# Key-mask tests split between products and maxima, and two stretches of a two-layer attention and expert kernel put in another order

## The chip, the cores and the metric

The kernel runs on one core of a Trainium2 chip. The metric is the device time of one execution in microseconds (us); lower is better. Shown are the median of three runs and one profiled execution.

## The reference

The input x holds 2 batches of 512 rows of 256 numbers, the context 2 batches of 1024 rows. Four steps follow each other, each added to x:

```python
x = x + attention0(layernorm(x), ctx, ctx, mask0, ...)   # 16 heads of 16, scores masked with -inf, softmax
x = x + experts0(layernorm(x), ...)                      # the best of 8 experts (256 -> 512 -> 256, GELU)
x = x + attention1(layernorm(x), ctx, ctx, mask1, ...)   # queries, keys, values normalised; bias -1e9 if masked
x = x + experts1(layernorm(x), ...)                      # shared expert (704 wide, SiLU) + the best 2 of 7
```

mask0 is 512 x 1024 int32, the same for both batches. mask1 is 2 x 512 x 1024, one byte each. In the inputs at hand both are nonzero for keys at the end of the context alone, the same for all 512 queries: keys 0 to 767 are masked away for every query (their entries are zero), and of the last 256 some are kept.

## The kernel before

All five engines run one program written out by hand: semaphores alone order them, and each engine and each DMA queue (SP's and ACT's) goes through its own list in order.

**Fast path and proof.** The kernel starts on the assumption that only the last FK = 256 keys of each batch count. While it computes, it proves this from the masks: `onesb` (all ones) times the mask rows on TensorE gives, for each key, how many of the 512 queries see it. The counts of keys 0 to 767 must be zero, those of the last 256 either 0 or 512 (`u = (512 - c) * c` must be zero), and some key must be left. The result is the flag on which all engines branch after step 3 of layer 0 (`branch`); in these inputs the fast path goes on.

**Start** (`sp_start`, `act_start`, `pe_start`, `dve_start`). SP's and ACT's queues issue the loads: halves of the keys `CTf` (ct_0, ct_1, 256 KB each), x tiles 0 to 3 (x0) and 4 to 7 (x1), weights `WP` (Wk, Wv, Wq), `cols` (14 KB), mask0 in two halves (m0_0, m0_1, 1 MB each), mask1 (1 MB). TensorE projects keys, turns the normalised x, projects queries and values, and counts mask0 in four plus four products of 512 columns (L524). VectorE does the statistics of x0, normalises two tiles, makes six small constants, casts both halves of mask0 to ones (L818), copies a turned half (L798) between the two, then does the statistics of x1, the values, and the row of mask values (`mval0`, L809) that SP spreads into `KT` (L589). `pe_first` begins with the scores (L890); it waits for `kt`, that row (`masked`) and `compact(1, 1)`.

**Attention** runs in 8 steps a layer, of 8 heads-by-batches each (`pe_step`, `dve_step`, `act_step`), every step in four gaps. In each step TensorE makes scores for the next step's maxima (L890), scores turned the other way for the exponentials (L900) and outputs (L921); VectorE takes 8 maxima (L1093), adds one turned maximum (L1099) and divides (L1107); ACT takes exponentials (L1260). The maxima go through a ring of three PSUM banks (`m_claim`: TensorE may write one when VectorE has freed the one three uses before). Other work is put beside: in layer 0 the counts of mask1, two products of 4 x 512 columns in each of steps 1 and 2 (`count0_0` to `count1_1`, L524), read by `dve_counts`; ACT's casts of mask1 (L704); and small VectorE work in pieces after each maximum (`late`): `key_counts_rest` for mask0 in step 1, for mask1 in steps 2 and 3.

**Shared expert of layer 1** (`shared_pe`, `shared_act`, `shared_dve`). It runs in CHUNKS = 12 chunks n, six to a batch: `shared_up(n)` (L1916), SiLU on ACT (L1946), the product on VectorE (`mul`, L1961), `shared_down(n - 1)` (L1927). The routing of the 7 experts is put beside the chunks (`beside1(n)` of the three engines): the last output of attention, statistics, turned rows, logits (L1579), `choose_experts`, ranks, `gates1`, `places1`, `tables1`. After the places POOL scatters the rows (16 indirect DMAs, L1747). Then come 19 tiles of routed experts (`tiles1`: up L2007, down L2022), whose up-weights SP loads (`load_up`, 1.4 MB each, three buffers) before it loads the scattered rows (`load_x`, L2797).

Of the kernel before, what the change touches and what calls it, by code (L numbers as in the profile page):

```python
# [5 lines left out]
F32 = mybir.dt.float32  # L6
# [11 lines left out]
NB = 2  # L18
# [40 lines left out]
def build(nc, A, out):  # L59
# [80 lines left out]
    fsum = sb("fsum", [128, 12], F32)  # L140
    junk = sb("junk", [128, 1], F32)
# [98 lines left out]
    def bank_uses():  # L240
        six, seven = [], []
        after = (["close1", "project1", "rows0_1", "x1_0", "q1_0"], ["rows1_1"])
        for l in range(NB):
# [12 lines left out]
            if l == 0:  # L256
# [13 lines left out]
    BESIDE_M = {(0, 0, 1): ["wg"], (0, 1, 1): ["count0_0"], (0, 1, 3): ["count0_1"], (0, 2, 1): ["count1_0"],  # L270
                (0, 2, 3): ["count1_1"], (0, 5, 1): ["close0_1"], (0, 5, 3): ["project0_0", "project0_1"],
# [249 lines left out]
    def key_counts_half(bank, b, mu, hf):  # L521

        for q in range(4):
            m = pe.matmul(PS[:, bank, :], onesb[:, :], mu[:, b * 4 + q, hf * 512:(hf + 1) * 512],  # L524
                          start=(q == 0), stop=(q == 3))
        return m

    def key_counts_pe(b, mu):

        key_counts_half(6, b, mu, 0)  # L530
        return key_counts_half(7, b, mu, 1)

    def key_counts_dve(n, c):

        flat = PS[:, 6:8, :].rearrange("p a n -> p (a n)")
        dve.tensor_reduce(fsum[:, n:n + 1], flat[:, 0:3 * FK], AX, ALU.add).then_inc(sem("counted"), 1)
        dve.tensor_copy(c, flat[:, 3 * FK:SK]).then_inc(sem("counted"), 1)

    def key_counts_rest(v, n, c, u):

        some, left, both = fsum[:, n:n + 1], fsum[:, 4 + n:5 + n], fsum[:, 7:8]
# [4 lines left out]
        settle(v, dve.tensor_reduce(fsum[:, 3:4], u, AX, ALU.add))  # L546
        yield
        settle(v, dve.tensor_tensor(some, some, fsum[:, 3:4], ALU.add))
        settle(v, dve.tensor_scalar(some, some, 0.0, None, ALU.is_equal))
        yield  # L550
        settle(v, dve.tensor_scalar(left, left, 0.0, None, ALU.is_gt))
        settle(v, dve.tensor_tensor(some, some, left, ALU.mult))
        if n:
            settle(v, dve.tensor_tensor(both, both, some, ALU.mult))
        else:
            settle(v, dve.tensor_copy(both, some))
        if n == 2:
            dve.tensor_copy(flags[:, 0:1], both).then_inc(sem("flag"), 1)
# [18 lines left out]
    def sp_start():  # L577
        load_keys0(sp, 0)
        sp.dma_start(X[:, 0:2, :], x_v[:, 0:2, :]).then_inc(sem("x0"), 16)
        sp.dma_start(WP[:, 1, :, :], A["L0_xattn_WvT"].rearrange("(k p) n -> p k n", p=128)).then_inc(sem("wp_1"), 16)  # L580
        load_mask0(sp, 0)
        sp.dma_start(X[:, 4:8, :], x_v[:, 4:8, :]).then_inc(sem("x1"), 16)
# [64 lines left out]
    def act_start():  # L647
        act.dma_start(WP[:, 0, :, :], A["L0_xattn_WkT"].rearrange("(k p) n -> p k n", p=128)).then_inc(sem("wp_0"), 16)
        act.dma_start(X[:, 2:4, :], x_v[:, 2:4, :]).then_inc(sem("x0"), 16)
        act.dma_start(cols[:, :, :], A["cols"]).then_inc(sem("col"), 16)  # L650
        load_keys0(act, 1)
        load_mask0(act, 1)
        act.dma_start(WP[:, 2, :, :], A["L0_xattn_WqT"].rearrange("(k p) n -> p k n", p=128)).then_inc(sem("wp_2"), 16)
# [4 lines left out]
        keys_compact(0)  # L658
# [3 lines left out]
        keys_compact(1)  # L662
# [18 lines left out]
        for f in range(2):  # L681
            queries_compact(2 + f, 3 + f)
            mask_cast(2 * f, 2 * f + 2)
# [18 lines left out]
    def mask_cast(q0, q1):  # L702
        for q in range(q0, q1):
            act.activation(mu1[:, q, :], m1i[:, q, :], ACT.Copy).then_inc(sem("mu1"), 1)  # L704
# [23 lines left out]
    def pe_start():  # L728
# [6 lines left out]
        def values_pair(j0):  # L735
            for j in (j0, j0 + 1):
                m = projected(4 + j // 2, j, 1, CTf, KCOLS[j])
            m.then_inc(sem("vals_ps"), 1)
# [5 lines left out]
        for b in range(NB):  # L744
            pe.wait_ge(sem(f"ct_{b}"), 16)
            for f in range(2):
                m = keys_half(f, b)
                if b:
                    m.then_inc(sem("k_ps"), 1)
        pe.wait_ge(sem("consts"), CONSTS)  # L750
# [3 lines left out]
        pe.wait_ge(*at(0, "wp_1", 16))  # L754
        values_pair(0)
# [3 lines left out]
        projected_T(0, 2, 0, XT[:, :, 0:512]).then_inc(sem("q_ps"), 1)  # L759
        pe.wait_ge(sem("mu0"), 2)  # L760
        key_counts_pe(0, mu0).then_inc(sem("count"), 1)
        projected_T(1, 2, 1, XT[:, :, 0:512]).then_inc(sem("q_ps"), 1)
        values_pair(2)

    def turn_second():

        pe.wait_ge(*at(0, "xn", 8))
        pe.wait_ge(sem("counted"), 3)
# [12 lines left out]
    def dve_start():  # L781
# [5 lines left out]
        for i in (0, 1):  # L787
            normal_dve("x0_0", i, XN[:, i, :], X[:, i, :]).then_inc(sem("xn"), 1)
        dve.wait_ge(sem("col"), 16)
# [2107 lines left out]
```

## Time and profile before

| | us |
|---|---|
| median of 3 runs | 516.57 (514.02 to 517.53) |
| the profiled execution | 517.48 |
| its span, first to last instruction | 516.2 |
| TensorE busy | 491.3 (95%) |
| VectorE busy | 258.8 (50%) |
| ACT busy | 201.4 (39%) |

Busy shares are means over stages with different limits. "idle before <-X" says how long the engine stood still before an instruction and whose end released it. Windows are in us from the start of the span. A matmul on float32 stands as two entries, so x8 are four matmuls.

### The profile page before, as it was taken

What the parts mean: (1) busy time and instruction counts of PE and PEld (TensorE: products, weight loads), DVE (VectorE), ACT (ScalarE), POOL (GpSimd) and SP (SyncE); (2) the same over time, 40 slices, a digit from 0 to 9 for tenths busy, and PEclk for the clock granted to TensorE, in tenths of its full rate; (3) what the DMA queues carried; (4) which work ended last, traced back from release to release, by engine and by line L of the source; (5) the groups of instructions that cost most, each with busy time, mean ns of one, the idle gap of its engine ahead of it and who ended that gap; (6) DMA issues with size and microseconds to landing.
All of it is one profiled execution on the core that took longest, in us unless ns stands there. A gap on an engine that the chain in (4) does not pass through costs nothing.

```text
span 516.2 us, 8825 instructions
## 1 busy us (share of the span) xinstructions
PE 491.3 (95%) x3290; PEld 368.5 (71%) x3293; DVE 258.8 (50%) x776; ACT 201.4 (39%) x416; POOL 85.2 (17%) x124
## 2 busy tenths in 40 slices
PE   6999999999999999999999899998999999999994
PEld 4555545648999887654654366565989999999993
DVE  4678897764474753876679352711313223223220
ACT  3747546452646445446465522301222222222221
POOL 2246000004020200200000000272021221221122
PEclk9999999999999999999999999998999999999999
DMA  8820009995132310480000300097676676676612
GB/s 297 237 66 2 2 13 341 367 356 180 42 102 64 102 32 22 125 283 2 1 0 2 117 6 1 21 360 247 223 260 184 228 254 190 220 257 191 218 21 27
DMA packets 43383, 73.13 MB, mean 142 GB/s; under 512 B 3553, under 2 KB 33729, under 8 KB 43332
## 3 DMA queue, kind: packets, MB, share of 16 engines
q1 hardware_dynamic: 34580, 60.47, 34.8%
q0 software_dynamic: 4336, 6.75, 5.9%
q10 hardware_dynamic: 4416, 5.26, 3.2%
q8 instruction: 29, 0.48, 0.4%
q14 instruction: 22, 0.18, 0.1%
HBM read 56.35 MB, written 14.51 MB: 137 GB/s over the span
## 4 chain that ended last, share of the span: by engine, by line
PE 78%; DVE 11%; DMA 5%; issue 2%; ACT 2%; POOL 1%; ACTq 0%; POOLq 0%; DVEq 0%
PE PS L2007 17%; PE PS L2022 9%; PE PS L890 9%; PE PS L1916 6%; PE PS L900 6%; PE PS L1789 5%; PE PS L1802 5%; PE PS L1927 4%; PE PS L921 3%; PE PS L402 3%; DVE W L1093 3%; PE PS L376 2%; DMA CT<-in_ctxT 2%; PE PS L909 2%; PE PS L381 1%
## 5 line engine op out<-in xcount | busy, mean ns | idle before, releaser
L1093 DVE TENSOR_REDUCE W<-PS 128x2 f32<-128x512 f32 x128 | 83.7, 686 | 34.8 <-PE PS L890 34.0
L2007 PE MATMUL PS<-PR,W 128*128 128x128 f32 x836 | 96.5, 275 | 0.0
L2007 PEld LDWEIGHTS PS<-PR,W 128*128 128x128 f32 x836 | 94.9, 192 | 0.1
L890 PE MATMUL PS<-W 32*128 32x256 f32 x512 | 83.1, 399 | 2.2 <-DVE W L1093 1.9
L900 PE MATMUL PS<-W 32*128 32x512 f32 x256 | 78.7, 638 | 0.2
L890 PEld LDWEIGHTS PS<-W 32*128 32x128 f32 x512 | 55.1, 184 | 24.8 <-issue 11.2
L2022 PE MATMUL PS<-W,PR 128*128 x228 | 52.5, 380 | 0.8 <-ACT PR L2739 0.8
L2790 POOL DMA_INDIRECT out<-PR,slots x19 | 29.7, 1563 | 131.9 <-ACT PR L2739 128.8
L1260 ACT ACTIVATE PR<-PS 128x512 f32<-128x512 f32 x64 | 35.2, 596 | 32.5 <-PE PS L900 32.4
L2022 PEld LDWEIGHTS PS<-W,PR 128*128 128x128 f32 x228 | 41.9, 190 | 6.1 <-issue 1.2
L1260 ACT ACTIVATE W<-PS 128x512 f32<-128x512 f32 x64 | 34.5, 598 | 22.0 <-PE PS L900 21.8
L2043 DVE TENSOR_TENSOR PR<-PR,PS 128x512 f32<-128x512 f32 x19 | 13.1, 688 | 58.8 <-PE PS L2007 58.8
L1916 PE MATMUL PS<-XT,W 128*128 128x512 f32 x88 | 40.1, 596 | 0.0
L900 PEld LDWEIGHTS PS<-W 32*128 32x128 f32 x256 | 24.1, 183 | 13.3 <-issue 6.6
L1789 PE MATMUL PS<-PR,W 128*128 128x128 f32 x256 | 31.6, 275 | 0.0
L1802 PE MATMUL PS<-W,PR 128*128 128x256 f32 x128 | 31.0, 382 | 0.0
L1789 PEld LDWEIGHTS PS<-PR,W 128*128 128x128 f32 x256 | 30.0, 192 | 0.3 <-issue 0.3
L1916 PEld LDWEIGHTS PS<-XT,W 128*128 128x128 f32 x88 | 16.2, 190 | 16.5 <-issue 16.1
L1927 PE MATMUL PS<-W,PR 128*128 128x256 f32 x96 | 24.4, 399 | 2.9 <-DVE PR L1961 1.9
L1927 PEld LDWEIGHTS PS<-W,PR 128*128 128x128 f32 x96 | 19.0, 200 | 11.0 <-issue 5.8
L1833 ACT ACTIVATE PR<-PS,b1c 128x128 f32<-128x128 f32 x64 | 18.3, 368 | 19.9 <-PE PS L1789 14.8
L1802 PEld LDWEIGHTS PS<-W,PR 128*128 128x128 f32 x128 | 23.0, 190 | 3.4 <-issue 1.0
(274 smaller groups left out, 591.0 us busy)
## 6 DMA issues: line engine op xcount, KB each, us to landing
W<-in_rguT SPq DMA_DIRECT2D x19, 1408.0 KB
W<-in_L_ffn_W SPq DMA_DIRECT2D x16, 512.0 KB, 9.6
W<-in_rdT SPq DMA_DIRECT2D x5, 768.0 KB, 11.2
scratch_rows<-W SPq DMA_DIRECT2D x1, 2860.0 KB
VR<-scratch_rows SPq DMA_DIRECT2D x19, 130.0 KB, 5.4
W<-in_mask SPq DMA_DIRECT2D x2, 1024.0 KB, 12.4
scratch_x<-W SPq DMA_DIRECT2D x1, 2048.0 KB, 14.2
PR<-scratch_x SPq DMA_DIRECT2D x16, 128.0 KB, 2.2
```

What stands on the lines that cost most here:

```text
L890: m = pe.matmul(PS[:, bank, q * FK:(q + 1) * FK], QT[r:r + 32, g, c:c + 128], KT[r:r + 32, g, b * FK:(b + 1) * FK], start=True, stop=True)
L900: pe.matmul(PS[:, bank, :], KT[r:r + 32, g, b * FK + kb * 128:b * FK + (kb + 1) * 128], QT[r:r + 32, g, 512 * b:512 * (b + 1)], start=True ...
L1093: dve.tensor_reduce(NM[:, s % 2, q:q + 2, c], PS[:, m_bank(use), :].rearrange("p (q n) -> p q n", q=2), AX, ALU.max).then_inc(sem("m_free" ...
L1260: act.activation(PX[s % 2][:, HEADS_W[k], :], PS[:, e_bank(use), :], ACT.Exp).then_inc(sem("e_free"), 1)
L1789: m = pe.matmul(PS[:, up_bank(i), j * 128:(j + 1) * 128], W[:, o:o + 128], XS0[:, i % 2, k, :], start=(k == 0), stop=(k == 1))
L1802: pe.matmul(PS[:, bk, 0:D], HT0[:, i % 2, j, :], W[:, o:o + D], start=(j == 0), stop=False)
L1833: act.activation(HT0[:, i % 2, j, :], PS[:, up_bank(i), j * 128:(j + 1) * 128], ACT.Gelu, bias=b1c[:, c:c + 1]).then_inc(sem("gelu"), 1)
L1916: m = pe.matmul(PS[:, 2 * (n % 2) + w, :], W[:, k * 2 * F1 + o:k * 2 * F1 + o + 128], XT[:, k, 512 * b:512 * b + 512], start=(k == 0), sto ...
L1927: m = pe.matmul(half(4 + t // 2, t), HS[:, n % 2, t * 128:(t + 1) * 128], W[:, o:o + D], start=(j == 0 and t % 2 == 0), stop=(j == NJ1 - 1 ...
L2007: m = pe.matmul(PS[:, bank, j * 128:(j + 1) * 128], W[:, o:o + 128], XS[:, r % 2, k, :], start=(k == 0), stop=(k == 1))
L2022: m = pe.matmul(PS[:, 6, 0:D], HT[:, r % 2, j, :], W[:, bass.ds(slot * SLOT + o, D)], start=(j == 0), stop=(j == NJ1 - 1))
L2790: ins = pool.indirect_dma_start(out, off, YO[:, r % 2, :], None, compute_op=ALU.add)
```

## The change

Three parts.

1. **Masks.** The products count the last 256 keys alone: mask0 in 4 products of 256 columns instead of 8 of 512, mask1 in 8 products of 256 columns in one place, step 2 gap 1 (`counts`), instead of 16 of 512 in four places. Keys 0 to 767 are tested on VectorE by maxima over the raw masks read as 32-bit words: 768 words of each of mask0's four row groups (two in the start, two in step 1), and 4 x 192 words for each batch of mask1 (step 1). 12 maxima a partition are made 0 or 1024 and join the counts by one more product, which adds to all counts and so breaks the test if any is nonzero. The casts shrink with the products: VectorE's to 2 x 256 numbers each, ACT's from eight of 1024 bytes to two of 4 x 256, both in the start. The small work on mask1 runs once, on 2 x 256 numbers, in step 3.
2. **Start.** SP's queue: ct_0, x tiles 0 and 1, ct_1, x1, m0_0. ACT's: Wk, cols, x tiles 2 and 3, Wv, Wq, m0_1. ACT normalises before it copies the projected keys. VectorE takes the statistics of x1 and copies the turned half before it casts masks. The values are projected one by one between other work. `turn_second` no longer waits for the counts to be read; `pe_first` does, later.
3. **Shared expert of layer 1.** The division of step 6 comes before chunk 0's product; the turned rows, logits and ranks of batch 1 move up by one chunk, `tables1` stays at chunk 5, after the places at 4. SP's second `load_up` waits for product 8, the third comes after the scattered rows' first two loads.

```diff
-    BESIDE_M = {(0, 0, 1): ["wg"], (0, 1, 1): ["count0_0"], (0, 1, 3): ["count0_1"], (0, 2, 1): ["count1_0"],
-                (0, 2, 3): ["count1_1"], (0, 5, 1): ["close0_1"], ...
+    BESIDE_M = {(0, 0, 1): ["wg"], (0, 2, 1): ["counts"], (0, 5, 1): ["close0_1"], ...
...
+    def key_counts(bank, c, mu, q0):
         for q in range(4):
+            m = pe.matmul(PS[:, bank, c:c + FK], onesb[:, :], mu[:, q0 + q, :], start=(q == 0), stop=(q == 3))
...
+    def first_keys0(v, q):
+        dve.tensor_reduce(first[:, q:q + 1], m0w[:, q, 0:SK - FK], AX, ALU.max).then_inc(*v.up())
+    def first_keys1(v, b):
+        dve.tensor_reduce(first[:, 4 + 4 * b:8 + 4 * b], m1w[:, 4 * b:4 * b + 4, 0:(SK - FK) // 4], AX, ALU.max).then_inc(*v.up())
+    def first_keys_late(v):
+        for q in (2, 3):
+            first_keys0(v, q)
+            yield
+        dve.wait_ge(sem("m1"), 16)
+        for b in range(NB):
+            first_keys1(v, b)
+            yield
+        dve.wait_ge(*v.now())
+        dve.tensor_scalar(firstb[:, :], first[:, :], 0.0, 1024.0, ALU.not_equal, ALU.mult).then_inc(sem("first_keys"), 1)
+        yield
+        yield from keys_alike(v, mc[0], mt[0], 0)
+    def keys_known(v):
+        dve.wait_ge(*m_freed("counts"))
+        yield from keys_alike(v, mc[1], mt[1], 1)
...
     def sp_start():
         load_keys0(sp, 0)
         sp.dma_start(X[:, 0:2, :], ...)
-        sp.dma_start(WP[:, 1, :, :], A["L0_xattn_WvT"]...)
+        load_keys0(sp, 1)
+        sp.dma_start(X[:, 4:8, :], x_v[:, 4:8, :]).then_inc(sem("x1"), 16)
         load_mask0(sp, 0)
-        sp.dma_start(X[:, 4:8, :], x_v[:, 4:8, :]).then_inc(sem("x1"), 16)
...
     def act_start():
...
-        keys_compact(0)
         act.wait_ge(sem("stats"), NORMS[True]["x0_0"])
         for i in (2, 3):
             normal_act("x0_0", i, XN[:, i, :], X[:, i, :]).then_inc(sem("xn"), 1)
-        keys_compact(1)
+        for f in range(2):
+            keys_compact(f)
...
+            elif (n, gap) == (2, 1):
+                pe.wait_ge(sem("mu1"), NB)
+                pe.wait_ge(sem("first_keys"), 1)
+                bank = m_claim("counts")
+                for b in range(NB):
+                    key_counts(bank, b * FK, mu1, 4 * b)
+                pe.matmul(PS[:, bank, 0:12], onesb[:, :], firstb[:, :], start=False, stop=True, ...
...
-            late = counts_rest(v, s - 2) if s > 1 else key_counts_rest(v, 0, mc[0][:, 0, :], mt[0]) if s else iter(())
+            late = first_keys_late(v) if s == 1 else keys_known(v) if s == 3 else iter(())
...
         def beside1(n):          # VectorE; TensorE and ACT move with it
             if n == 0:
-                dve_divide(1, 6, v)
                 dve_divide(1, 7, v)
...
-            elif n == 3:
+            elif n == 2:
                 dve_xt("rows1_1", 1)
-            elif n == 4:
+            elif n == 3:
                 ... logits1_1, choose_experts(v, 2)
-            elif n == 5:
+            elif n == 4:
                 gates1(v)
                 ... places1(v, ...)
+            elif n == 5:
                 whole(tables1(v))
+        dve_divide(1, 6, v)
         shared_dve(beside1)
...
-            for r in range(UPS):
-                load_up(r)
+            load_up(0)
+            sp.wait_ge(sem("mul"), CHUNKS - 4)
+            load_up(1)
             sp.wait_ge(sem("scattered"), SCATTERED[2])
             load_x(0)
             load_x(1)
+            load_up(2)
```

## Rows read from the trace of the kernel before

**Rows 1.** The page's chain that ended last, share of the span by engine.
```profile
PE 78%; DVE 11%; DMA 5%; issue 2%; ACT 2%; POOL 1%; ACTq 0%; POOLq 0%; DVEq 0%
```

**Rows 2.** Windows of all engines: busy us (x instructions), PEclk, DMA share, GB/s.
```profile
48.18:54.25 6.07, 5.82 (x44) 3.25 (x48) 5.83 (x15) 4.09 (x8) 4.72 (x7) 1.00 0.00 0
54.25:59.18 4.93, 4.93 (x45) 2.58 (x48) 3.80 (x10) 2.10 (x5) 0.00 (x0) 1.00 0.01 2
79.24:83.20 3.96, 3.96 (x40) 2.21 (x44) 3.75 (x7) 2.88 (x6) 0.00 (x0) 1.00 0.96 301
```

**Rows 3.** Windows of VectorE alone, from a step's first maximum to the next step's.
```profile
46.30:57.10 10.80, 9.63 (x21) 1.00 0.00 1
57.10:68.10 11.00, 9.82 (x24) 1.00 0.01 1
68.10:77.29 9.19, 8.53 (x22) 1.00 0.05 13
```

**Rows 4.** DMA issues of the start: KB each, us from issue to landing.
```profile
X<-in_x SPq DMA_DIRECT2D x1, 512.0 KB, 13.4
WP<-in_L_xattn_WvT SPq DMA_DIRECT2D x1, 256.0 KB, 6.2
CT<-in_ctxT ACTq DMA_DIRECT2D x1, 256.0 KB, 8.8
```

**Rows 5.** Timeline of the start: start us, us, instruction, idle before.
```profile
5.64 3.78 PE L731 MATMUL PS<-CT,WP 128*128 128x256 f32 x8 [1.68 <-DMA WP<-in_L_xattn_WkT]
...
11.20 1.99 PE L731 MATMUL PS<-CT,WP 128*128 128x256 f32 x8 [1.78 <-DMA CT<-in_ctxT]
...
12.95 1.08 ACT L473 ACTIVATE PR<-X,NW 128x256 f32<-128x256 f32 x2
...
16.81 1.88 PE L381 MATMUL PS<-XT,WP 128*128 128x512 f32 x4
...
20.91 0.72 SPq L589 DMA_DIRECT2D W<-W  x1
...
23.99 1.14 PE L890 MATMUL PS<-W 32*128 32x256 f32 x8
```

**Rows 6.** VectorE up to 80 us by line and form: count, busy us, mean ns.
```profile
L818 DVE TENSOR_SCALAR W<-W 128x2048 bf16<-128x2048 int32 x2 | 2.4, 1219 | 0.0
L546 DVE TENSOR_REDUCE fsum<-W 128x1 f32<-128x256 f32 x3 | 1.3, 420 | 0.1
L536 DVE TENSOR_REDUCE fsum<-PS 128x1 f32<-128x768 f32 x1 | 0.9, 947 | 0.0
```

**Rows 7.** Timeline of the shared expert of layer 1.
```profile
296.07 0.63 PE L934 MATMUL PS<-ident,W 128*128 128x128 f32 x4 [1.57 <-DVE W L1107]
...
334.94 2.93 SPq L515 DMA_DIRECT2D W<-in_rguT  x3
...
335.38 1.97 PE L1927 MATMUL PS<-W,PR 128*128 128x256 f32 x8 [0.96 <-DVE X L1968]
...
345.77 1.89 PE L1927 MATMUL PS<-W,PR 128*128 128x256 f32 x8
...
355.08 1.07 ACT L1946 ACTIVATE PR<-PS 128x512 f32<-128x512 f32 x2 [10.05 <-PE PS L1916]
...
356.45 2.69 PE L1927 MATMUL PS<-W,PR 128*128 128x256 f32 x8 [1.92 <-DVE PR L1961]
```

**Rows 8.** Windows of the same stretch, columns as in rows 2.
```profile
348.00:352.00 4.00, 4.00 (x13) 2.21 (x12) 0.00 (x0) 0.00 (x0) 3.08 (x4) 1.00 0.98 394
358.00:360.00 2.00, 2.00 (x7) 1.52 (x6) 0.39 (x2) 0.00 (x0) 0.00 (x0) 0.50 0.97 260
```

**Rows 9.** Windows of VectorE: logits and choice, gates and places, tables. Columns as in rows 3.
```profile
321.72:325.10 3.38, 2.96 (x16) 1.00 0.00 0
328.50:331.95 3.45, 3.00 (x21) 1.00 0.00 0
331.95:333.45 1.50, 1.33 (x9) 1.00 0.00 0
```

More of the change, by code:

```diff
@@ L140, in build @@
     fsum = sb("fsum", [128, 12], F32)
+    first = sb("first", [128, 12], F32)
+    firstb = sb("firstb", [128, 12], BF16)
     junk = sb("junk", [128, 1], F32)
@@ L517, in load_up, with keys_alike @@
                      ).then_inc(sem(f"up_w_{r % UPS}"), 16)
-    def key_counts_half(bank, b, mu, hf):
+    def key_counts(bank, c, mu, q0):
         for q in range(4):
-            m = pe.matmul(PS[:, bank, :], onesb[:, :], mu[:, b * 4 + q, hf * 512:(hf + 1) * 512],
-                          start=(q == 0), stop=(q == 3))
-        return m
[L528 to L541, printed above, removed]
+            m = pe.matmul(PS[:, bank, c:c + FK], onesb[:, :], mu[:, q0 + q, :], start=(q == 0), stop=(q == 3))
+        return m
+    def keys_alike(v, c, u, n0):
+        n = c.shape[1]
+        some, left = fsum[:, n0:n0 + n], fsum[:, 4 + n0:4 + n0 + n]
         dve.tensor_scalar(u, c, -1.0, 512.0, ALU.mult, ALU.add).then_inc(*v.up())
@@ L700, in queries_compact, with mask_cast @@
                        ).then_inc(sem("compact"), 1)
-    def mask_cast(q0, q1):
-        for q in range(q0, q1):
-            act.activation(mu1[:, q, :], m1i[:, q, :], ACT.Copy).then_inc(sem("mu1"), 1)
+    def mask_cast(b):
+        act.activation(mu1[:, 4 * b:4 * b + 4, :], m1i[:, 4 * b:4 * b + 4, SK - FK:SK], ACT.Copy).then_inc(sem("mu1"), 1)
     def load_keys0(q, b):
@@ L733, in keys_half, with values_of @@
             return m
[L735 to L738, printed above, removed]
+        def values_of(j):
+            m = projected(4 + j // 2, j, 1, CTf, KCOLS[j])
+            if j % 2:
+                m.then_inc(sem("vals_ps"), 1)
         pe.wait_ge(sem("consts"), 2)
@@ L759, in pe_start @@
         projected_T(0, 2, 0, XT[:, :, 0:512]).then_inc(sem("q_ps"), 1)
+        values_of(2)
         pe.wait_ge(sem("mu0"), 2)
[L761 removed]
+        key_counts(7, FK, mu0, 0).then_inc(sem("count"), 1)
         projected_T(1, 2, 1, XT[:, :, 0:512]).then_inc(sem("q_ps"), 1)
[L763 removed]
+        values_of(3)
     def turn_second():
         pe.wait_ge(*at(0, "xn", 8))
[L768 removed]
         for k, bank in ((0, 3), (1, 6)):
@@ L788, in dve_start @@
             normal_dve("x0_0", i, XN[:, i, :], X[:, i, :]).then_inc(sem("xn"), 1)
+        dve.wait_ge(sem("x1"), 16)
+        for t in range(4):
+            dve.bn_stats(ST[:, COLUMN["x0_1"] + t, :], X[:, 4 + t, :]).then_inc(*v.up())
+        dve.wait_ge(*v.now())
+        for t in range(COLUMN["x0_1"], COLUMN["x0_1"] + 4):
+            dve.bn_aggr(MV[:, t, :], ST[:, t, :]).then_inc(sem("aggregated"), 1)
+        dve.wait_ge(*at(0, "turned", 2))
+        dve.tensor_copy(XT[:, 1, 0:512], PS[:, 3, :]).then_inc(sem("xt"), 1)
+        mask0_ones(0)
         dve.wait_ge(sem("col"), 16)
@@ L1185, in dve_beside @@
                 dve_wg()
-            elif n in (1, 2) and gap in (1, 3):
-                dve_counts(n - 1, gap // 2)
+            elif (n, gap) == (2, 1):
+                dve.wait_ge(*m_full("counts"))
+                dve.tensor_copy(masked1[:, :, :], PS[:, m_bank("counts"), :].rearrange("p (b n) -> p b n", b=NB)
+                                ).then_inc(sem("m_free"), 1)
             elif (n, gap) == (5, 1):
@@ L1314, in act_beside @@
         if l == 0:
-            if n < 2 and gap in (0, 2):
-                q = 4 + 2 * n + gap // 2
-                mask_cast(q, q + 1)
-            elif (n, gap) == (5, 1):
+            if (n, gap) == (5, 1):
                 act_xt_ring("close0", 0)
```

84 lines of the change are left out of this document (30 added, 54 removed).

## The prediction, made before the changed kernel was run

> **What bounds the kernel now.** I read the chain that ended last first, to see which engine sets the end: TensorE carries 78% of it [rows 1]. A change pays where it takes work from TensorE or closes a hole in it, and elsewhere not at all. Then I went through the three stretches that are touched.
>
> *Start*, by the timeline. TensorE projects the first half of the keys from 5.64 and stands still until the second half lands at 11.15 (8.8 after issue) [rows 4, 5]. ACT has the projected keys ahead of its two tiles to normalise in its list, so these run at 12.95; from there one chain leads over the turned rows and their copy to the first queries (16.81), the counts, the row of mask values (issued 20.91) and the first scores at 23.99 [rows 5].
>
> *Steps 1 to 3 of layer 0*, by windows between the outputs (L921). A half step takes 3.96 in step 4; in steps 1 and 2 it takes 6.07 and 4.93 in turn [rows 2]. The 4.93 is 3.96 and 0.97 of count products. The 6.07 has 1.1 more, with VectorE busy 5.83 of 6.07: VectorE, not TensorE, holds that half. VectorE needs 10.8, 11.0 and 9.2 from step to step, with 9.63, 9.82 and 8.53 busy [rows 3], where the two halves of TensorE's alone would be 7.9.
>
> *Shared expert of layer 1.* TensorE waits 1.57 for a division that VectorE could have made before, and 0.96 for VectorE, which did gates, places and tables in one go between two products [rows 7]. Then a hole: TensorE ends its up products of the last but one chunk at about 351, but ACT, which stood idle 10.05, takes the SiLU at 355.08. TensorE waits 1.92 and then runs two down products at 2.7 each (one is shown) where one takes 1.89 [rows 7]; the granted clock is 0.50 there, 1.2 GHz, the lower of its two levels, after it had stood still [rows 8]. No semaphore that the list names explains ACT's wait. What stands beside it: the three up-weight loads, issued from 334.94, with the scatters, keep the DMA share at 0.98 until 352, and ACT goes on when that is over [rows 7, 8]. I take it that something ACT needs is late behind them; the profile doesn't show what.
>
> **Part 1, start.** ct_1 becomes third on SP's queue, where Wv was, and Wv landed 6.2 after issue, at 8.0 [rows 4]: TensorE goes from the first half (until 9.42) straight to the second and ends about 11.3. ACT normalises when the statistics are there (about 11.5, right before VectorE's own two tiles) instead of 12.95, so the turned rows are ready at 13.7 instead of 15.2. VectorE now has the statistics of x1 ahead of the copy: four passes over 256 numbers, at 0.42 as the 256-number operation [rows 6], and four tiny ones, some 1.8 with overlap. Does x1 land in time? It landed 13.4 after issue behind a mask of 1 MB [rows 4]; now 0.79 MB of small rows are ahead of it. Third place lands at 8.0, two more such places at that pace (2 us each) make 12.0; I take 12.3, bounds 11 and the old 16.2. Then the copy runs at 14.1 and the queries at 14.8 instead of 16.81: 2.0 won. Behind them count products of 4 x 256 instead of 8 x 512 columns (0.5 instead of 1.7); masks have landed by about 15.5, their casts (2 x 512 numbers instead of 2 x 2048 in 1.22 [rows 6]) take 0.4 each. Now ACT's list is late next: presets, first queries at 17.6, presets, second queries done at 21.2 (before 22.9), and SP, which sends those first queries before the mask row: that row goes out at about 19.6 instead of 20.91 [rows 5], still behind mask1's megabyte, and lands near 22.2. So scores begin at 22.2 instead of 23.99: **1.8** gained; bounds 0.5 (x1 late, or the second key half still at the slow rate of the first, 3.78 instead of 1.99 [rows 5]) and 2.8 (TensorE's own list is through at 21.2). Two maxima of 768 words stand before VectorE's first score maximum: they end at about 21.7, hidden under the wait for scores; without it they would cost 1.9.
>
> **Part 2, steps 1 to 3.** TensorE loses 4 x 0.97 and gains 8 products of 256 columns and a short one, about 1.0: 2.9 less. But VectorE is what is late. It has no row of a maximum over 32-bit integers from SBUF; nearest are 768 numbers from PSUM, 0.947, and 256 from SBUF, 0.420 [rows 6]. 512 more numbers at the slope of those two give the same, 0.95, which I take; the lower bound is half of it, the upper 3 (a form without a fast path). Step 1 gets four of them, 3.7 with overlap, in place of `dve_counts` (one read of 512, two of 256 numbers: 0.69 + 2 x 0.42 = 1.5) and of the 10.8 - 9.6 = 1.2 it stood idle, nearly all of that on counts [rows 3]; 0.5 of idle time stays, and so does the small work on mask0. 10.8 + 3.7 - 1.5 - 1.2 makes 11.8 at the most; the overlap of short operations makes me take 11.3, 0.5 more. Step 2 loses its small work (four operations on 256 numbers and six tiny ones, 2.7) and `dve_counts` (1.5), and gets one copy of 512 (0.69): from 9.8 busy VectorE falls to 6.3, and TensorE sets 7.9 + 1.0 = 8.9, 2.1 less than 11.0. Step 3 has its small work on 512 instead of 256 numbers, four operations longer by 0.13 to 0.27, and two more tiny ones with their waits: 0.9 to 1.0 more. Sum -0.5 + 2.1 - 0.9 = 0.7; as the late start of step 2 is partly caught up, **1.0**, bounds -2 and 2.9. ACT's six casts less lie beside exponentials that wait for TensorE: nothing. If the maxima ran at their lower bound, 1.8 more would come.
>
> The Trainium skill weighs against this part: "VectorE: DVE Perf Modes", § The perf-mode tier table, gives `tensor_reduce` one number per cycle whatever the type, and calls it the slowest of VectorE's operations; by that rule the part would cost time wherever VectorE sets the pace, as it does in step 1. The slope of rows 6, 0.53 for 512 numbers, agrees with it. The same page, § The TRN2 errata, has a fixed cost of 58 cycles from SBUF against 120 from PSUM; by that each maximum would be 0.86 and step 1 0.35 shorter, with 1.3 as the part's sum. The rows show no such gap between the two memories.
>
> **Part 3, shared expert and loads.** The division (0.7) moves under chunk 0's up products: 1.57 gone. Everything in chunk 0 and 1 then starts 1.5 earlier. Splitting the routing: logits and choice (3.4) under chunk 4's products, gates and places (3.5) under chunk 5's, tables (1.5) before chunk 6's product [rows 9]. Even the longer two with a product of 0.7 are shorter than a chunk's 5.2 (its down products 1.89 [rows 7] and up products of twice that, less overlap), so no down product waits, and 0.96 goes too. **2.5**, bounds 1.6 and 2.6. The scatters start some 9 us earlier (places at 323 instead of 332), which nobody waits for but the row loads.
>
> The second up load leaves at product 8 (about 334), the third after the scatters (about 345): the first is through before 334, the second by about 340, so the DMA is not full when ACT should take the late SiLUs. If that was the cause, the 1.92 and twice 0.85 of slow clock go: **3.6**. SP's list puts the row loads behind the scatters as before; the weights of the third tile arrive about 352, 15 us before use. What is left then is the row load behind the fourth up load, some 1 us, unchanged.
>
> **Sum.** 1.8 + 1.0 + 2.5 + 3.6 = 8.9. Against the profiled execution (517.5, span 516.2) 508.6; against the median of the runs, 0.9 lower, 507.7. I say 508.2.
>
> **Rivals.** (a) *ACT's hole stays*: its cause is not the loads, or it moves to another place (the third load now runs from 345 to 351, beside the same SiLUs). For it: the lists show no link; against it: ACT went on within 3 us of the DMA falling quiet. 508.2 + 3.6 = 511.8. (b) *The start gives nothing*: x1 lands at 14 to 16, VectorE stands before the copy, the queries start at 17 to 18. Loss up to 2.5: 510 to 510.7. For it: ACT's mask of long rows takes bandwidth from SP's short ones, as SP's mask did from ct_1 before; against it: it is issued last. (c) *The maxima are slow*, the other side. Six are added, two with 1.4 us of cover. At p us each they cost 6(p - 0.95) - 1.4. All gain is gone at p = 2.7, and from 3.5 on the kernel is over 1% slower; at 3.8 it would take 524. Against it: the casts read 2048 integers in 1.22 [rows 6], so integers as such aren't slow. (d) *VectorE in steps 1 to 3* loses 2 instead of winning 1 because the pieces fall between maxima the ring waits for: 511.2.
>
> **Chances.** Forecast within 2 us either way 0.50; better than that 0.06; (a) 0.18; (b) 0.08; (d) 0.08; two of these together, 513 to 516, 0.06; (c) 0.04. The range of 8 in 10 runs from 505.0 to 512.8. A measurement tells about 1% (5.2 us) from no change. Faster by more, under 511.4: the forecast, the better case, (b), half of (d), a third of (a): 0.72. Slower 0.04, same 0.24.
>
> **What would show it.** Scores (L890) begin near 22.2, and the mask row's issue near 19.6. The 768-word maxima take 0.9 to 1.0. From one step's first maximum to the next: 11.3, under 9, 10.1. The product count at L524's place occurs once, in step 2. TensorE waits before neither the last turned output nor chunk 6's down product. ACT takes chunk 10's SiLU within 1 us of its up products, and the granted clock stays 1.00 there. From the first scores' gain on, the distance between the kernels is 1.8, about 2.8 after step 3, 5.3 at chunk 6 and 8.9 at the first routed tile. The forecast is wrong if the maxima cost over 1.5 or ACT's hole is still there.

## The result, and the profile after

| | before | after |
|---|---|---|
| median of 20 runs each, us | 514.2 (513.2 to 517.5) | 510.92 (508.46 to 522.64) |
| ratio | | 0.9923, 95% interval 0.9905 to 0.9942 |
| the profiled execution, us | 517.48 | 509.93 |
| its span | 516.2 | 508.6 |
| mean granted TensorE clock in the profiled execution | 0.995 | 0.995 |

The change gains 0.8% (about 4.0 us), where I forecast 508.2 from 516.57, that is 1.6%. The median of after lies in the range, 2.7 above the forecast. Two things stand out before any experiment. The profiled execution of before lies 3.3 above the median of its 20 runs, so a part of what I summed up from it was not there to be won in most executions. And after has a tail that before, with 513.2 to 517.5, did not have: 10 of its 20 executions have a mean granted clock under 0.99, and they take 511.5 to 522.6. The ratio leaves the most disturbed of them out; medians and counts below take in all.

*Start.* This is TensorE's timeline of after (start, duration, what, idle time before and what ended it), with SyncE's issue of the row of mask values.

```profile
5.23 5.20 PE L744 MATMUL PS<-CT,WP 128*128 128x256 f32 x16 [1.27 <-DMA WP<-in_L_xattn_WkT]
...
13.27 1.06 PE L379 MATMUL PS<-ident,PR 128*128 128x128 f32 x8 [1.38 <-ACT PR L476]
...
15.22 1.95 PE L384 MATMUL PS<-XT,WP 128*128 128x512 f32 x4
...
20.03 1.03 PE L405 MATMUL PS<-WP,CT 128*128 128x256 f32 x4
22.86 1.14 PE L907 MATMUL PS<-W 32*128 32x256 f32 x8 [1.80 <-DMA W<-W]
```
```profile
19.70 0.72 SPq L603 DMA_DIRECT2D W<-W  x1
```

The keys run through in one go, the turned rows come at 13.27 instead of 14.18, the queries at 15.22 instead of 16.81 [rows 5]. The row of mask values goes out at 19.70, but its chain entry is 3.07 long, so the scores begin at 22.86 and not at 22.2: 1.13 gained against 23.99. New is that TensorE stands still for 1.80 before them: its own work is through earlier, since the count products are short.

*Steps 1 to 3.* VectorE's new operations (name, shapes, count, busy us, mean ns), and the windows from one step's first maximum to the next; columns are length, then busy time of PE, PEld, DVE, ACT and POOL, granted clock, DMA share, GB/s.

```profile
L547 DVE TENSOR_REDUCE first<-W 128x1 f32<-128x768 uint32 x4 | 3.8, 944 | 0.0
L551 DVE TENSOR_REDUCE first<-W 128x4 f32<-128x768 uint32 x2 | 1.9, 942 | 0.0
```
```profile
45.18:56.21 11.03, 10.71 (x75) 6.03 (x76) 10.82 (x22) 6.14 (x11) 6.14 (x12) 1.00 0.00 0
56.21:65.12 8.91, 8.91 (x78) 5.10 (x76) 6.93 (x12) 3.85 (x7) 0.00 (x0) 1.00 0.01 3
65.12:75.71 10.59, 9.40 (x73) 5.36 (x74) 9.33 (x21) 5.07 (x10) 0.00 (x0) 1.00 0.14 49
```

The maxima cost 0.94 as forecast. The steps take 11.03, 8.91 and 10.59, together 30.53, against 30.99 before [rows 3]: 0.46 gained.

*Shared expert of layer 1.* ACT takes every SiLU 5.16 after the one before, and TensorE goes into the routed tiles without a hole.

```profile
339.30 0.60 ACT L1948 ACTIVATE PR<-PS 128x512 f32<-128x512 f32 x1 [4.56 <-PE PS L1918]
344.46 0.60 ACT L1948 ACTIVATE PR<-PS 128x512 f32<-128x512 f32 x1 [4.56 <-PE PS L1918]
349.62 0.59 ACT L1948 ACTIVATE PR<-PS 64x512 f32<-64x512 f32 x1 [4.56 <-PE PS L1918]
```
```profile
351.60 1.99 PE L1929 MATMUL PS<-W,PR 128*128 128x256 f32 x8
...
353.65 5.08 PE L2009 MATMUL PS<-PR,W 128*128 128x128 f32 x44
359.45 0.44 PE L2720 MATMUL PS<-ident,VR 128*128 128x128 f32 x2 [0.72 <-DMA VR<-scratch_rows]
```

The distance between the two profiles is 1.13 at the first scores, 1.6 after step 3, 1.9 at the first up products, 4.95 from chunk 8's up products on, 8.5 at the first routed tile, and 7.6 at the end. Of the 0.9 lost there 0.4 are waits for row loads in the first tiles (0.72 and 0.28, against 0.59 in before); the rest I did not follow.

### The profile page after: what moved, and what is told of

The parts are those of the page before. It is cut to its first block, busy times and chain, and to the rows that moved or that the text cites. A ratio compares the mean times of both kernels' runs of the same rounds, so it can differ in the third digit from the quotient of the medians.

```text
span 508.6 us, 8775 instructions
## 1 busy us (share of the span) xinstructions
PE 487.9 (96%) x3282; PEld 368.3 (72%) x3282; DVE 257.3 (51%) x764; ACT 195.6 (38%) x410; POOL 85.8 (17%) x124
## 4 chain that ended last, share of the span: by engine, by line
PE 73%; DVE 13%; DMA 5%; issue 3%; ACT 3%; POOL 1%; ACTq 0%; SPq 0%; POOLq 0%; DVEq 0%
PE PS L2009 17%; PE PS L2024 9%; PE PS L907 8%; PE PS L1918 8%; PE PS L917 5%; PE PS L405 4%; DVE W L1115 4%; PE PS L1929 4%; PE PS L938 4%; PE PS L1804 3%; PE PS L1791 3%; PE PS L379 2%; PE PS L926 2%; DMA VR<-scratch_rows 1%; PE PS L1581 1%
## 5 line engine op out<-in xcount | busy, mean ns | idle before, releaser
L907 PE MATMUL PS<-W 32*128 32x256 f32 x512 | 85.0, 402 | 4.2 <-DVE W L1115 2.4
L907 PEld LDWEIGHTS PS<-W 32*128 32x128 f32 x512 | 56.8, 186 | 28.6 <-issue 13.3
L1265 ACT ACTIVATE PR<-PS 128x512 f32<-128x512 f32 x64 | 35.1, 595 | 33.6 <-PE PS L917 33.5
L2024 PEld LDWEIGHTS PS<-W,PR 128*128 128x128 f32 x228 | 41.9, 190 | 6.1 <-issue 1.2
L917 PEld LDWEIGHTS PS<-W 32*128 32x128 f32 x256 | 24.2, 184 | 12.8 <-issue 6.2
L1804 PE MATMUL PS<-W,PR 128*128 128x256 f32 x128 | 31.0, 382 | 0.0
L1804 PEld LDWEIGHTS PS<-W,PR 128*128 128x128 f32 x128 | 23.0, 190 | 3.4 <-issue 1.0
L2034 ACT ACTIVATE PR<-PS 128x512 f32<-128x512 f32 x19 | 11.3, 597 | 33.6 <-PE PS L2009 33.6
L2036 ACT ACTIVATE PR<-PS 128x128 f32<-128x128 f32 x19 | 5.3, 277 | 48.1 <-PE PS L2009 48.1
```

What stands on the lines that cost most here:

```text
L907: m = pe.matmul(PS[:, bank, q * FK:(q + 1) * FK], QT[r:r + 32, g, c:c + 128], KT[r:r + 32, g, b * FK:(b + 1) * FK], start=True, stop=True)
L917: pe.matmul(PS[:, bank, :], KT[r:r + 32, g, b * FK + kb * 128:b * FK + (kb + 1) * 128], QT[r:r + 32, g, 512 * b:512 * (b + 1)], start=True ...
L1265: act.activation(PX[s % 2][:, HEADS_W[k], :], PS[:, e_bank(use), :], ACT.Exp).then_inc(sem("e_free"), 1)
L1804: pe.matmul(PS[:, bk, 0:D], HT0[:, i % 2, j, :], W[:, o:o + D], start=(j == 0), stop=False)
L2024: m = pe.matmul(PS[:, 6, 0:D], HT[:, r % 2, j, :], W[:, bass.ds(slot * SLOT + o, D)], start=(j == 0), stop=(j == NJ1 - 1))
```

## The experiments

Kernels of one group ran beside the same runs of before: `order_only`, `loads_only`, `p3_only` and `p12_only` (before 515.71), `masks_only`, `warm_start`, `fill_counts` and `after_again` (516.55), `start_p3`, `warm_fill` and `p3_again` (517.15). The ratios are to before in the same group, with 95% intervals; the first group ran on another chip than the other two. The last column has the same count for before in the group.

| kernel | median us (runs) | ratio | executions with mean clock under 0.99 | before beside it |
|---|---|---|---|---|
| `order_only` | 511.72 (6) | 0.9921 (0.9897 to 0.9944) | 0 of 6 | 1 of 25 |
| `loads_only` | 517.15 (12) | 1.0037 (1.0013 to 1.0062) | 3 of 12 | 1 of 25 |
| `p3_only` | 510.14 (8) | 0.9921 (0.9893 to 0.9948) | 0 of 8 | 1 of 25 |
| `p3_again` | 513.77 (12) | 0.9920 (0.9890 to 0.9949) | 5 of 12 | 1 of 16 |
| `p12_only` | 517.34 (12) | 1.0037 (1.0010 to 1.0065) | 7 of 12 | 1 of 25 |
| `masks_only` | 518.01 (12) | 1.0000 (0.9967 to 1.0032) | 8 of 12 | 4 of 19 |
| `after_again` | 512.90 (6) | 0.9923 (0.9897 to 0.9949) | 4 of 6 | 4 of 19 |
| `warm_start` | 511.90 (6) | 0.9890 (0.9848 to 0.9932) | 3 of 6 | 4 of 19 |
| `fill_counts` | 512.53 (7) | 0.9914 (0.9884 to 0.9945) | 2 of 7 | 4 of 19 |
| `warm_fill` | 511.82 (6) | 0.9893 (0.9853 to 0.9933) | 0 of 6 | 1 of 16 |
| `start_p3` | 511.07 (6) | 0.9875 (0.9839 to 0.9911) | 0 of 6 | 1 of 16 |
| before, all groups | | | 6 of 60 | |

### Which part carries the gain

`p3_only`: before with part 3. `order_only`: before with part 3 but for the loads. `loads_only`: before with only

```
-            for r in range(UPS):
-                load_up(r)
+            load_up(0)
+            sp.wait_ge(sem("mul"), CHUNKS - 4)
+            load_up(1)
             sp.wait_ge(sem("scattered"), SCATTERED[2])
             load_x(0)
             load_x(1)
+            load_up(2)
```

`p12_only`: after with part 3 undone.

> The kernel before with part 3 alone (order of the shared expert and of the up loads). Theory 1 (the forecast's terms hold, but ACT's hole is in only some executions): ratio about 0.990, some 5 us less than before: 2.5 from the two waits, about half of 3.6 from the hole; profile without the 1.57, the 0.96 and the hole. Theory 2 (the hole is there in every execution): 6.1 less, ratio 0.988. Theory 3 (the wide spread upward of the changed kernel comes from part 3): times spread over 10 us and the granted clock below 0.99 in half of them.

> The kernel before with the new order of division, rows, logits, ranks and tables alone; the three up loads still go out together. Theory 1 (loads make ACT's hole): 2.5 less, ratio 0.995, and ACT stands still for some us in the last chunks, now where scatters and loads overlap. Rival (the hole hangs on the late scatters): hole gone, ratio 0.988.

> The kernel before with the up loads sent one by one alone. Theory 1 (three loads at once make ACT's hole): the two waits of 1.57 and 0.96 stay, hole gone: 3.6 less than the profiled execution of before, and 1 to 3.6 less in the ratio, by how often before has the hole. Rival (the hole has another cause): no difference in the ratio, and the hole is there in a profile.

> The changed kernel with part 3 undone (start and masks stay). Theory 1: 1.1 from the start and 0.5 from steps 1 to 3 are kept: 1.6 less than before, ratio 0.997. Theory 3a (the spread upward and the low granted clock come from the start or the masks): spread and clocks as in the changed kernel, 0.97 to 0.99 in half the runs; rival: clocks of 0.99 and more and a spread of 4 us as before.

Part 3 gives the whole 0.8% (0.9921, a smaller gain than either 0.990 or 0.988), and all of that comes from the order of the work, 0.9921 again, between the 0.995 and the 0.988 of its two theories; the order of the loads gives nothing (it measures 0.4% slower alone, and with the order the ratio is the same, though the medians, 511.72 and 510.14, are 1.6 apart). Parts 1 and 2 together, from which I had expected 2.8 us, cost 0.4% in these runs, although the profiled execution of `p12_only` has a span of 512.7, 3.5 under before's (1.9 of that is ACT's hole, which cost less there; see the table below): 7 of its 12 executions have a clock of 0.981 to 0.988 and take 516.9 to 520.3.

ACT's hole tells why the loads don't matter. These are ACT's rows of `loads_only`, then of `order_only`, and the issue of the first row loads, which wait for the scatters, in both.

```profile
344.72 0.60 ACT L1946 ACTIVATE PR<-PS 128x512 f32<-128x512 f32 x1 [4.56 <-PE PS L1916]
353.87 0.60 ACT L1946 ACTIVATE PR<-PS 128x512 f32<-128x512 f32 x1 [8.56 <-remote]
```
```profile
338.27 0.60 ACT L1946 ACTIVATE PR<-PS 128x512 f32<-128x512 f32 x1 [5.23 <-PE PS L1916]
347.52 1.09 ACT L1946 ACTIVATE PR<-PS 128x512 f32<-128x512 f32 x2 [8.65 <-remote]
353.08 0.59 ACT L1946 ACTIVATE PR<-PS 64x512 f32<-64x512 f32 x1 [4.48 <-PE PS L1916]
```
```profile
354.21 0.82 SPq L2797 DMA_DIRECT2D VR<-scratch_rows  x2
```
```profile
347.03 9.23 SPq L2798 DMA_DIRECT2D VR<-scratch_rows  x3
```

The hole is still there in both. (Between two full chunks ACT waits 4.56 as a rule; what is above that is the hole.) In `loads_only` it ends at 353.87, and TensorE waits 1.10 for the product; in `order_only` it ends at 347.52 and costs TensorE nothing. The scatters run 8 us earlier there, so the hole falls on chunk 9's SiLU, and chunk 10 has 3.4 us of up products to cover it. In before it falls on chunk 10's, and chunk 11, with half the rows, has 1.9. In both kernels ACT goes on within 0.5 us of the moment when the scatters are through and the row loads go out.

What the hole costs differs from one execution to the next, and so does part 3's gain in a pair of profiles. Times from TensorE's first up product of the shared expert to its last, and from there to the first routed tile, us:

| profile | first to last up product | last up product to first routed tile | TensorE's wait for chunk 10's product |
|---|---|---|---|
| before | 61.86 | 9.47 | 1.92, then down products of 2.7 at a lower clock |
| `loads_only` | 61.86 | 6.98 | 1.10 |
| `masks_only` | 61.87 | 7.56 | 1.69 |
| `p12_only` | 61.86 | 7.59 | 1.71 |
| the nine with part 3's order, without `late_scatter` | 58.79 to 58.81 | 5.94 to 5.95 | none |

The order gives 3.05 everywhere. The hole, of which I had reckoned 3.6, cost 3.5 in before's profile alone, where the granted clock was 0.50 behind it [rows 8]; in the three others, whose down products behind the wait take 2.00, it cost 1.0 to 1.6. 3.05 with these makes 4.1 to 4.7, beside the 4.1 that the ratio 0.9921 says.

### What ACT's hole hangs on

In the profiled executions of before and of eleven other runs ACT has this gap of 8.6 to 10.1, and goes on between 0.3 before and 1.1 after the row loads' issue. Only the first profiled execution of after has none; `after_again`, the same program, has it (337.07 to 347.02). So its absence there was chance. `late_scatter` is `start_p3` (below) with the scatters held back:

```
         tokens1()
+        pool.wait_ge(sem("mul"), CHUNKS)
         scatter(2)
```

> The kernel with parts 1 and 3 and the old masks; GpSimd sends layer 1's scatters only when the last product of the shared expert is made (about 352 instead of 323). Theory S (ACT stands still in the shared expert because of the scatters: in twelve of thirteen profiled executions it went on within 1.2 us of their end): ACT takes every SiLU of the shared expert within 5.3 us of the one before, no gap of 9 to 10; TensorE then waits some 20 us for the rows and the whole takes 525 to 535. Rival U (ACT's hole comes from the up loads or from ACT's own list): a gap of 9 to 10 us stays at chunk 9 or 10, before any scatter has been sent.

It took 542.15, in one execution, with before at 516.92 beside it. ACT's SiLUs stand 5.16 apart up to the last, and the scatters begin at 358.95:

```profile
346.42 0.60 ACT L1948 ACTIVATE PR<-PS 128x512 f32<-128x512 f32 x1 [4.56 <-PE PS L1918]
351.58 0.60 ACT L1948 ACTIVATE PR<-PS 128x512 f32<-128x512 f32 x1 [4.56 <-PE PS L1918]
356.74 0.59 ACT L1948 ACTIVATE PR<-PS 64x512 f32<-64x512 f32 x1 [4.56 <-PE PS L1918]
```
```profile
358.95 1.00 POOL L1749 DMA_INDIRECT scratch_rows<-CT,posi  x1 [125.91 <-DVE PR L1963]
```

Without scatters beside it there is no hole. Together with the ends that move with the scatters' end (from 345 to 361 us, by kernel) this speaks for the scatters; since one execution of after had scatters and no hole, one without it is not proof. What in the scatters holds ACT is not in the profile: it calls the releaser "remote" in nine of the twelve and a product of TensorE in the other three, and in the kernel the semaphores that ACT waits for there (`up_g`, `down1`) are TensorE's. `late_scatter` was some 7 us slower than theory S had said: TensorE stood still for 24.68 instead of 20 and went on at half its clock (below), and its clock was down for another stretch in layer 1's attention, here in windows:

```profile
253.00:266.00 13.00, 13.00 (x58) 7.00 (x58) 4.67 (x8) 2.36 (x5) 0.00 (x0) 0.50 0.00 1
```

### What lowers the clock

`masks_only` is before with part 2 alone. `warm_start` is after with 14 products nobody reads, ahead of the first scores:

```
     def pe_first():
+        for n in range(14):
+            pe.matmul(PS[:, 6, 0:FK], onesb[:, :], mu0[:, n % 4, :], start=True, stop=True)
         pe.wait_ge(*at(0, "kt", 48))
```

`fill_counts` is after with 8 such products in three places of steps 1 to 3, and `warm_fill` has both, with 16 products in the first place:

```
         bank = m_claim(use)
+        if (l, s, i) in ((0, 3, 0), (0, 3, 4), (0, 4, 4)):
+            pe.wait_ge(sem("mu1"), NB)
+            for n in range(8):
+                pe.matmul(PS[:, bank, 0:FK], onesb[:, :], mu1[:, n, :], start=True, stop=True)
```

> The kernel before with part 2 alone: its own order of transfers and of the start's work, its own shared expert, but products over the last 256 keys, maxima, small casts. With parts 1 and 2 together half of the executions had a mean granted clock of 0.981 to 0.988 and took 517 to 520. Theory A (the count products that were taken out of steps 1 to 3 kept TensorE busy while VectorE sets the pace; without them the clock falls in some executions): the low clocks are here too, median 516 to 518. Theory B (TensorE's wait of 1.8 us before the first scores lets the clock fall): that wait is not here, clocks 0.99 to 0.999 and a median 0.5 to 2 us under before.

> The changed kernel with 14 products of 256 columns (some 1.6 us) that nobody reads, while TensorE waits for the row of mask values. Theory B: the spread upward goes, clocks over 0.99, median about 509.5. Theory A: as the changed kernel, 509 to 522 with clocks down to 0.97.

> The changed kernel with three groups of 8 products of 256 columns that nobody reads, before score products of steps 1 to 3, where the count products that were taken out stood: TensorE has the same 2.9 us of work again. Theory A: the spread upward goes, clocks over 0.99, fastest run 0 to 2.9 us slower than the changed kernel's, median at or below its 510.9. Theory B: spread and clocks stay and everything is up to 2.9 slower.

> The changed kernel as it is, on the same chip as the other three. Both theories: fastest 508.5 to 509.5, about half of the runs above 511 with a mean granted clock below 0.99.

> The changed kernel with both fillings: 16 products of 256 columns in the wait before the first scores and three times 8 in steps 1 to 3, none of them read. Theory A and B together: no run with a mean clock below 0.99, all within 3 us of the fastest, median 509 to 511. If low clocks stay in a third of the runs or more, idle time of TensorE in these two places is not their whole cause.

Theory B named a wait that `masks_only` would not have. It has one: its first scores wait too (1.59 idle, at 26.03), since there too the count products are short. So that kernel could not tell A from B, and the profiles have to. Windows of `masks_only`, `after_again`, `fill_counts` and `warm_fill` around the first scores, columns as above (length, then busy time of PE, PEld, DVE, ACT and POOL, granted clock, DMA share, GB/s):

```profile
24.00:26.00 2.00, 0.43 (x3) 0.04 (x2) 1.46 (x3) 1.09 (x2) 0.40 (x2) 1.00 0.48 97
26.00:28.00 2.00, 1.97 (x13) 1.67 (x14) 0.98 (x3) 0.00 (x0) 0.00 (x0) 0.80 0.34 82
28.00:32.00 4.00, 3.23 (x19) 2.16 (x18) 2.23 (x4) 0.60 (x1) 0.66 (x3) 0.67 0.25 69
```
```profile
21.00:23.00 2.00, 0.21 (x3) 0.14 (x3) 0.69 (x1) 1.14 (x3) 0.00 (x0) 1.00 0.52 115
23.00:24.00 1.00, 1.00 (x9) 0.67 (x9) 0.00 (x0) 0.00 (x0) 0.00 (x0) 0.98 0.66 144
24.00:27.00 3.00, 3.00 (x18) 2.53 (x20) 1.98 (x3) 0.60 (x1) 0.00 (x0) 0.50 0.14 24
```
```profile
21.00:23.00 2.00, 0.03 (x2) 0.06 (x2) 0.53 (x1) 0.97 (x2) 0.00 (x0) 1.00 0.59 139
23.00:26.00 3.00, 3.00 (x15) 2.34 (x16) 1.29 (x2) 0.23 (x1) 0.00 (x0) 0.57 0.29 55
26.00:32.00 6.00, 5.24 (x20) 3.08 (x19) 3.44 (x6) 0.36 (x1) 3.47 (x7) 0.50 0.14 45
32.00:40.00 8.00, 8.00 (x16) 3.05 (x14) 1.79 (x4) 1.63 (x2) 2.55 (x3) 0.50 0.02 4
```
```profile
21.00:23.00 2.00, 1.65 (x16) 1.24 (x14) 0.48 (x1) 0.93 (x2) 0.00 (x0) 1.00 0.62 144
23.00:24.00 1.00, 0.97 (x8) 0.77 (x8) 0.00 (x0) 0.00 (x0) 0.00 (x0) 1.00 0.50 107
24.00:27.00 3.00, 2.63 (x22) 1.92 (x20) 2.60 (x5) 0.60 (x1) 0.00 (x0) 1.00 0.14 16
```

In the first three TensorE stands nearly still for 1.6 to 2.0 us (0.03 to 0.43 busy of 2), and within some 2 us of going on it is at 0.50, 1.2 GHz. In `fill_counts` that lasted until after 40; its profiled execution took 522.08 where its fastest took 510.42. Of five profiled executions with such a wait three show the fall there; of the nine others none does between 20 and 28 (`warm_fill` has a short fall behind 28).

Over the executions: with short count products and nothing in their place 29 of 50 have a mean clock under 0.99 (after 10 of 20, `after_again` 4, `p12_only` 7, `masks_only` 8). With the old count products it is 14 of 104. It holds within the groups too: 7 of 12 against 4 of 51 in the first, 12 of 18 against before's 4 of 19 in the second. So the tail grows with part 2, though part 2 isn't its only source: part 3 alone had 0 of 8 in the first group and 5 of 12 in the third. With the wait filled it is 3 of 6, where theory B had none, with the steps filled 2 of 7, where theory A had none; neither filling takes the tail away alone, as far as six or seven executions can tell. With both it is 0 of 6, but the third group has no kernel with part 2 and nothing filled to set beside it. That both together take it away is likely, not shown, and which of the two places matters more stays open. `after_again` gave the same ratio as after, 0.9923, but its fastest execution, 511.37, is slower than the 508.5 to 509.5 that both theories had. Falls come elsewhere too, with and without part 2: near 220, in layer 1's attention, in five of the profiles, two of them with the old masks (`fill_counts`, which runs 10 behind there, has one at 234). Leaving out the executions under 0.99, the medians are 509.65 instead of 510.92 (after) and 514.71 instead of 517.34 (`p12_only`): by that estimate the tail costs 1.3 to 2.6 us of median, more than the 0.46 that steps 1 to 3 save.

### Parts 1 and 3 without part 2

`start_p3` is before with parts 1 and 3; masks, casts and count products are before's, and nothing takes maxima.

> The kernel before with parts 1 and 3, and its own masks: full count products, full casts, no maxima. Theory C (part 1 gives its 1.1 us in every execution, and what costs is part 2, by the idle time of TensorE before the first scores and by lighter steps 1 to 3): first scores at 22.5 to 23.2 with no idle time of TensorE over 1 us before them, mean granted clocks of 0.99 and more, 0.5 to 1.5 us faster than parts 2 and 3 without it, ratio 0.987 to 0.991. Rival D (any earlier start brings the low clocks): clocks below 0.99 in half of the runs.

> Part 3 alone again, beside the two others: ratio 0.992 as before, clocks of 0.99 and more, 1 to 1.5 us slower than the kernel with parts 1 and 3 if theory C holds, equal if part 1 gives nothing.

Theory C holds so far: 0 of 6 under 0.99, ratio 0.9875, the lowest of all, 0.45% under part 3 alone beside it, which missed its "clocks of 0.99 and more" with 5 of 12. The intervals still overlap, and against after (0.9923) too, so neither difference is shown; the point estimates say 2.3 us for part 1 and 2.5 us lost by part 2. Its first scores:

```profile
21.31 1.03 PE L402 MATMUL PS<-WP,CT 128*128 128x256 f32 x4
23.33 1.14 PE L892 MATMUL PS<-W 32*128 32x256 f32 x8 [0.99 <-DMA W<-W]
```

The long count products fill 1 us of the wait and cost 0.5 against after's 22.86. That part 1 may give more than the 1.1 of the two profiles has a likely reason in the keys. First of `p3_only`, then of `order_only`, which have the same start:

```profile
11.13 2.00 PE L731 MATMUL PS<-CT,WP 128*128 128x256 f32 x8 [2.08 <-DMA CT<-in_ctxT]
```
```profile
11.01 3.78 PE L731 MATMUL PS<-CT,WP 128*128 128x256 f32 x8 [2.04 <-DMA CT<-in_ctxT]
```

After the wait for the second half of the keys TensorE projects it in 2.0 or in 3.8. The six profiles with the old transfers have 1.99, 1.99 and 2.00, and 3.15, 3.78 and 3.78; their first scores begin at 23.9 to 24.1, and 24.5 to 26.0. In the eight with the new ones there is no wait, the products of both halves (x16) take 4.0 to 6.3 in one go, and the first scores begin at 22.9 to 23.4 in all of them. Before's profiled execution was one of the lucky ones [rows 5]. The mean of the six is 24.7, some 1.4 behind the 23.3 and 23.4 of the two new starts with the old masks. The profiles don't carry this to the end: `start_p3` has its first scores 0.6 before `p3_only`'s 23.92, but its span, 510.2, is 1.7 longer than `p3_only`'s, so the 2.3 rest on the ratios alone.

## Why the forecast came out as it did

- **The base.** The sum, 8.9, was made against 517.48 and carried over to a median of three runs, 516.57. The median of 20 was 514.2. Profile against profile the gain is 7.55; in the ratio it is 4.0. I had treated what one execution shows as being there in all. All profiles of before's order have ACT's hole, but its price in this one was 3.5, and 1.6 in the two others with the same code in that stretch (7.56 and 7.59 against 9.47): this is about 1.9 of the 3.3. The rest isn't settled; the waits for row loads vary (0 to 2.1 us by profile), and the second half of the keys was a fast one here, so it isn't that.
- **Start, 1.8 forecast, 1.13 in the profiles.** Transfers, keys, turned rows and the mask row's issue (19.70 for 19.6) came as worked out. The term that failed is the landing of that row, 3.07 after its issue where I had reckoned 2.6, behind mask1's megabyte. What I did not look at was the other side: I wrote that TensorE's own list is through at 21.2 and took the second between that and the scores as free. It is 1.80 long, and in three of the five profiles with such a wait the clock falls behind it.
- **Steps 1 to 3, 1.0 forecast, 0.46 in the profiles.** Maximum 0.95 and 0.944; step 1 11.3 and 11.03; step 2 8.9 and 8.91; step 3 10.1 and 10.59, where the small work on 512 numbers was undersized by 0.5. The Trainium skill's rule ("VectorE: DVE Perf Modes", § The perf-mode tier table: one number per cycle for `tensor_reduce`, whatever its type) agrees with the trace: 0.944 for 768 words of 32 bits from SBUF, 0.947 for as many float32 from PSUM, and 0.524 more than 256 numbers take [rows 6]. The 0.86 that I estimated from the same page's errata section is not what the row shows. Rival (c), slow maxima, is out. No rival had the thing that did happen: that with less work for TensorE in the start and in these steps more executions have a lower clock.
- **Order in the shared expert, 2.5 forecast, 3.05 in the profiles** (4.95 - 1.9). Both waits are gone. `order_only` shows that this edit is the change: the 61.86 from the first to the last up product are 58.80 in it.
- **ACT's hole, 3.6 forecast, 3.5 in the profiles, for the wrong reason.** I put the hole down to three up loads at once and the gain to their being spread. `loads_only` has the hole and no gain. The hole goes with the scatters, and what the change does is to move these 8 us up, where a full chunk covers ACT's standstill. Rival (a) had half of it: the hole stays, at another place; but its price there is nothing, not 3.6. That the sum came near here is luck of one execution, before's 3.5; in the three others of that order the price is 1.0 to 1.6, and a ratio takes the mean of such prices. By my own sign, that the forecast is wrong if ACT's hole is still there, this step of it was wrong: the hole is there in all other profiles with part 3 beside the scatters.
- **Row loads.** I wrote that their wait, about 1 us, would be unchanged. After has 0.72 and 0.28 in the first tiles, before 0.59; the distance falls from 8.5 to 7.6, and 0.4 of that is this. Profile against profile the sum's terms then stand as 1.1 + 0.5 + 0.3 (between step 3 and the shared expert, not forecast) + 3.05 + 3.5 - 0.9 = 7.6.
- **Chances.** I gave 0.72 to faster by over 1% and 0.24 to within 1%; the measured 0.8% is the latter (the cases that I listed for the former add up to 0.74). The range held, by errors of both signs: the base 2.4 too high, the gain 4.9 too large (8.9 against 4.0), which two causes explain in the main: the hole's usual price, some 2 less than the 3.6, and parts 1 and 2, for which I had 2.8, the profiles 1.6 and the ratios nothing.

## What to carry over

Make the sum from a stretch's rows, but before a hole is counted as won ask in how many executions it is there, and what else ends when it ends: here a hole's end moved with the scatters and not with the loads that ran beside it. Where another engine sets the pace, work taken from TensorE gains little there (0.46 here) and can cost its clock; look at the idle time that a cut leaves in front of the next product, and keep the cheap products if the wait behind them is there anyway. If two engines pass work back and forth, a late one costs only what the chunk that follows can't cover: put it before a long chunk, not before the short last one.

## What the runs showed of the hardware

TensorE's clock after standing still, in `late_scatter`, which waits 24.68 us for rows (columns as above):

```profile
350.00:358.00 8.00, 8.00 (x27) 4.92 (x26) 0.71 (x2) 1.78 (x3) 0.00 (x0) 1.00 0.01 3
358.00:362.00 4.00, 0.43 (x3) 0.03 (x1) 0.67 (x1) 0.00 (x0) 2.44 (x3) 1.00 0.54 186
362.00:383.00 21.00, 0.00 (x0) 0.00 (x0) 0.00 (x0) 0.00 (x0) 12.97 (x14) 0.50 0.31 102
383.00:386.00 3.00, 2.89 (x8) 2.44 (x9) 1.10 (x5) 0.00 (x0) 0.00 (x0) 0.50 1.09 374
386.00:392.00 6.00, 5.84 (x50) 5.50 (x49) 2.31 (x4) 0.72 (x2) 0.00 (x0) 0.99 0.91 342
```

It is at 1.00 while TensorE has just gone idle, at 0.50 until 386, 3 us after TensorE has work again, and then at 0.99. The down products of one chunk (x8) took 3.12 in that stretch instead of 1.89.

At the start of the program the granted clock can't be read off the profile so simply. Windows of `p3_only`, `order_only` and `loads_only`, whose second half of the keys took 2.00, 3.78 and 3.15:

```profile
12.00:16.00 4.00, 3.02 (x19) 2.47 (x18) 2.23 (x7) 2.83 (x5) 0.00 (x0) 1.00 1.07 363
12.00:16.00 4.00, 3.86 (x12) 2.79 (x11) 1.34 (x3) 2.35 (x4) 0.00 (x0) 1.00 1.07 362
12.00:16.00 4.00, 3.86 (x16) 2.88 (x15) 1.69 (x6) 2.95 (x5) 0.00 (x0) 0.61 1.07 361
```

The same products take 2.00 and 3.78 where the row says 1.00 in both, and 3.15 where it says 0.61. That the clock was low in the second as well is likely from the duration, but no row shows it.

ScalarE can stand still on a semaphore that TensorE has already raised, while GpSimd's scatters to memory run. Its idle time was 8.6 to 10.1 where 4.56 is usual, and the SiLU came 4.0 to 5.7 later than it could have, an estimate from TensorE's rows: with no hole it follows the begin of its chunk's up products by 1.92. It did so in twelve of the thirteen profiled executions with the scatters beside the shared expert, and in the one with them moved behind it, it didn't. The cause behind it stays open.
